# Combining pass of a sandwich layer: six buffers for the sums, loads two tiles ahead, and the inverse deviation taken as a ScalarE root and a VectorE reciprocal in place of GpSimd's power

## What is computed

```python
x = x + layernorm(mixer(layernorm(x)))            # first pass, gives x1
# experts: 8, two of them for each token, and a shared one
y = einsum('etd,te->td', experts(layernorm(x)), gate_dense) + shared(layernorm(x))
x = x + layernorm(y)                              # the second part is the combining pass
# layernorm: (x - mean) / sqrt(var + 1e-5), over the 256 channels
```

## Time and profile before

| what | us |
|---|---|
| median of three runs | 1092.72 |
| lowest and highest of the three | 1087.05, 1095.67 |
| the profiled execution's own time | 1095.33 |
| its span (first to last instruction) | 1093.5 |
| combining pass within the span | 1018.3 to 1093.5 |

### The profile page before, as it was taken

The page is one execution under the profiler, slowest core; times in us unless marked ns, Lnnn a source line. Parts: engine busy times, 40 slices in busy tenths (PEclk is TensorE's granted clock), DMA queues, the critical chain, the costliest instruction groups (busy, mean ns, idle before and its releaser), DMA issues. The chain is left out here.

```text
span 1093.5 us, 23369 instructions
## 1 busy us (share of the span) xinstructions
PE 978.0 (89%) x6344; PEld 874.3 (80%) x6344; DVE 863.2 (79%) x2223; ACT 574.5 (53%) x1045; POOL 763.3 (70%) x763
## 2 busy tenths in 40 slices
PE   4577999999999999999998979999999999997552
PEld 3466888888888888888887869899999999997331
DVE  5779999989989999899878657667777676666686
ACT  5335667556755765576555524344444443443465
POOL 3665787787778777877786634577776676667488
PEclk9879999999999999999999999999999999999555
DMA  6150453345334533443441476987787878986797
GB/s 218 40 161 31 141 165 106 124 142 163 90 132 149 158 94 133 149 143 100 143 131 54 141 258 134 257 181 117 116 171 156 213 120 211 224 200 85 254 395 287
DMA packets 107894, 171.93 MB, mean 157 GB/s; under 512 B 13870, under 2 KB 75977, under 8 KB 107593
## 3 DMA queue, kind: packets, MB, share of 16 engines
q1 hardware_dynamic: 76120, 119.68, 34.4%
q0 software_dynamic: 26976, 35.93, 18.8%
q10 hardware_dynamic: 4752, 15.80, 3.7%
HBM read 173.53 MB, written 76.08 MB: 228 GB/s over the span
## 5 line engine op out<-in xcount | busy, mean ns | idle before, releaser
L2063 POOL DMA_INDIRECT sum_y<-e_y,e_row_at x142 | 223.8, 1576 | 43.3 <-issue 39.8
L1897 PE MATMUL e_h_ps<-e_z_hi,w_room 128*128 128x256 f32 x1136 | 217.2, 284 | 11.6 <-DMA w_room<-w_split 9.4
L1897 PEld LDWEIGHTS e_h_ps<-e_z_hi,w_room 128*128 128x128 f32 x1136 | 181.8, 191 | 15.1 <-issue 13.4
L1941 ACT ACTIVATE e_act_h<-e_h_ps,w_room 128x256 f32<-128x256 f32 x142 | 67.4, 474 | 192.8 <-PE e_h_ps L1897 154.2
L1897 PE MATMUL e_h_ps<-e_z_lo,w_room 128*128 128x256 f32 x568 | 160.0, 282 | 0.0
L1647 POOL DMA_INDIRECT slots_x<-f_xf,f_at x120 | 127.6, 1063 | 29.0 <-issue 29.0
L1913 PE MATMUL e_y_ps<-w_room,e_h_hi 128*128 128x256 f32 x568 | 117.9, 291 | 1.8 <-DVE e_h_lo L1987 1.1
L1980 DVE SCALAR_TENSOR_TENSOR e_h<-e_h_ps,w_room,e_act_h 128x256 f32<-128x256 f32 x142 | 68.1, 482 | 61.8 <-ACT e_act_h L1941 48.6
L1172 DVE RECIPROCAL f_den<-f_den 128x256 f32<-128x256 f32 (+1 forms) x49 | 109.2, 2234 | 0.6
L1897 PEld LDWEIGHTS e_h_ps<-e_z_lo,w_room 128*128 128x128 f32 x568 | 108.5, 191 | 0.0
L651 PE MATMUL f_h_ps<-f_f_hi,f_w_hi 128*128 128x512 f32 x224 | 91.8, 410 | 6.0 <-DVE f_h_room L1208 3.2
(11 more groups left out here) (301 smaller groups left out, 2964.6 us busy)
## 6 DMA issues: line engine op xcount, KB each, us to landing
w_room<-w_split SPq DMA_DIRECT2D x73, 512.0 KB
w_room<-w_split SPq DMA_DIRECT2D x71, 514.0 KB
w_room<-w_split ACTq DMA_DIRECT2D x69, 512.0 KB
rows_room<-slots_x SPq DMA_DIRECT2D x71, 260.0 KB
f_x_in<-x SPq DMA_DIRECT2D x16, 512.0 KB, 5.2
f_x_res<-x SPq DMA_DIRECT2D x16, 512.0 KB, 4.6
x_dram<-f_x_room SPq DMA_DIRECT2D x16, 512.0 KB, 2.9
c_acc<-sum_y SPq DMA_DIRECT2D x16, 512.0 KB, 7.6
```

The source lines that it names most:

```text
L1897: last = pe.matmul(h_ps[q][:, which, :], w13(p, q, part)[:, which, c, :], z[p % 2][:, c, :], start=(n == 0), stop=(n == 5))
L1941: act.activation(act_h[q][:, :], h_ps[q][:, 0, :], ACT.Silu, bias=bias(p, 0, q)).then_inc(silu_ready, 1)
L2063: pool.indirect_dma_start(out=dst[:, :], out_offset=bass.IndirectOffsetOnAxis(ap=row_at[p][:, j:j + 1], axis=0), in_=y[p][:, j, :], in_off ...
```

## The change

All of it lies in `combine`, but for one tile and the names of semaphores in what comes before.

- `acc` has six buffers (`DEPTH`), `x1` and `res` have four (`X_DEPTH`). SyncE's queue first fetches `acc` of tiles 0 and 1, then in turn i `acc` of tile i+2 and `x1` of tile i. The load of `acc[s]` waits until tile s-6 is normalised.
- ScalarE takes `std = Sqrt(var + eps)` in a new `deviation`, which stands in turn i for tile i+1, between `gates_turned(i + 2)` and `normalise(i)`.
- VectorE takes the reciprocal and the offset in a new `scales`. Its turn i is `add(i)`, `scales(i - 1)`, `measure(i)`. Minus the mean and the variance plus epsilon as instructions of their own are gone.
- GpSimd keeps `add_x1` alone.
- `eps`, a 128 x 1 tile, is set by VectorE at the start of the expert stage; two semaphores there (`own_ready`, `gates_split`) become one (`prepared`).

```diff
-    DEPTH = 4
+    DEPTH, X_DEPTH = 6, 4
...
-            for i in range(tiles):
+            def load_acc(i):
+                if not inside(i, tiles):
+                    return
                 wait(sp, normed, i - DEPTH + 1)
                 sp.dma_start(acc[i % DEPTH][:, :, :], rows(acc_dram, i)).then_inc(acc_loaded[i % DEPTH], 16)
-                wait(sp, res_ready, i - DEPTH + 1)
-                sp.dma_start(x1[i % DEPTH][:, :, :], rows(x1_dram, i)).then_inc(x1_loaded[i % DEPTH], 16)
+            def load_x1(i):
+                wait(sp, res_ready, i - X_DEPTH + 1)
+                sp.dma_start(x1[i % X_DEPTH][:, :, :], rows(x1_dram, i)).then_inc(x1_loaded[i % X_DEPTH], 16)
+            for i in range(DEPTH - X_DEPTH):
+                load_acc(i)
+            for i in range(tiles):
+                load_acc(i + DEPTH - X_DEPTH)
+                load_x1(i)
...
+            def deviation(s):
+                if not inside(s, tiles):
+                    return
+                act.wait_ge(moments_ready, s + 1)
+                wait(act, rstd_ready, s - 1)
+                act.activation(std[s % 2][:, :], moments[s % 2][:, :, 1], ACT.Sqrt, bias=eps[:, :]).then_inc(std_ready, 1)
             for i in range(-2, tiles + 2):
                 gates_turned(i + 2)
+                deviation(i + 1)
                 normalise(i)
                 store(i - 1)
...
-                dve.wait_ge(moments_ready, s + 1)
-                wait(dve, offset_ready, s - 1)
-                dve.tensor_scalar(minus_mean[s % 2][:, :], moments[s % 2][:, :, 0], -1.0, None, ALU.mult)
-                dve.tensor_scalar(var[s % 2][:, :], moments[s % 2][:, :, 1], EPS, None, ALU.add)\
-                    .then_inc(var_ready, 1)
-            for i in range(tiles):
-                add(i)
+            def scales(s):
+                if not inside(s, tiles):
+                    return
+                dve.wait_ge(std_ready, s + 1)
+                wait(dve, normed, s - 1)
+                dve.reciprocal(rstd[s % 2][:, :], std[s % 2][:, :]).then_inc(rstd_ready, 1)
+                dve.wait_ge(rstd_ready, s + 1)
+                dve.scalar_tensor_tensor(out=offset[s % 2][:, :], in0=moments[s % 2][:, :, 0], scalar=-1.0,
+                                         in1=rstd[s % 2][:, :], op0=ALU.mult, op1=ALU.mult).then_inc(offset_ready, 1)
+            for i in range(tiles + 1):
+                if i < tiles:
+                    add(i)
+                scales(i - 1)
+                if i < tiles:
+                    measure(i)
...
-                pool.tensor_tensor(rstd[s % 2][:, :], var[s % 2][:, :], minus_half[:, :], ALU.pow)\
-                    .then_inc(rstd_ready, 1)
-                pool.wait_ge(rstd_ready, s + 1)
-                pool.tensor_tensor(offset[s % 2][:, :], minus_mean[s % 2][:, :], rstd[s % 2][:, :], ALU.mult)\
-                    .then_inc(offset_ready, 1)
...
-            for i in range(tiles + 1):
-                inverse_std(i)
-                add_x1(i - 1)
+            for i in range(tiles):
+                add_x1(i)
```

More of the change, by code:

```diff
@@ L1961, in _ @@
         def _(dve):
+            dve.memset(ahead["eps"][:, :], EPS)
             dve.tensor_tensor(own[:, :, :], tile_of["start"][:, :, None].to_broadcast([P, tiles, SUBS]),
-                              own_s[:, None, :].to_broadcast([P, tiles, SUBS]), ALU.add).then_inc(own_ready, 1)
+                              own_s[:, None, :].to_broadcast([P, tiles, SUBS]), ALU.add).then_inc(prepared, 1)
             for p in range(2):
                 dve.tensor_scalar(spare_row[p][:, :], own_s[:, :], float(TOKENS + p * T), None, ALU.add)\
-                    .then_inc(own_ready, 1)
-            dve.wait_ge(own_ready, 3)
+                    .then_inc(prepared, 1)
+            dve.wait_ge(prepared, 3)
             def low(s, p):
@@ L2095, in combine @@
         eye, b_out, b_ready = (ahead[n] for n in ("eye", "b_out", "b_ready"))
-        minus_half = sb("minus_half", [P, SUBS])
+        eps = ahead["eps"]
         gt = [sb(f"gt{p}", [G, T], F32R) for p in range(2)]
         acc = [sb(f"acc{p}", [P, SUBS, C]) for p in range(DEPTH)]
-        x1 = [sb(f"x1{p}", [P, SUBS, C]) for p in range(DEPTH)]
+        x1 = [sb(f"x1{p}", [P, SUBS, C]) for p in range(X_DEPTH)]
         normal = [sb(f"normal{p}", [P, SUBS, C]) for p in range(2)]
-        res = [sb(f"res{p}", [P, SUBS, C]) for p in range(DEPTH)]
+        res = [sb(f"res{p}", [P, SUBS, C]) for p in range(X_DEPTH)]
         stats = [sb(f"stats{p}", [P, SUBS, 6]) for p in range(2)]
         moments = [sb(f"moments{p}", [P, SUBS, 2]) for p in range(2)]
-        var = [sb(f"var{p}", [P, SUBS]) for p in range(2)]
-        minus_mean = [sb(f"minus_mean{p}", [P, SUBS]) for p in range(2)]
+        std = [sb(f"std{p}", [P, SUBS]) for p in range(2)]
         rstd = [sb(f"rstd{p}", [P, SUBS]) for p in range(2)]
@@ L2109, in combine @@
         b_ps = [ctx.enter_context(nc.psum_tensor(f"c_b_ps{p}", [P, SUBS, C], F32)) for p in range(2)]
-        x1_loaded = [sem(f"x1_loaded{p}") for p in range(DEPTH)]
-        half_ready = sem("half_ready")
+        x1_loaded = [sem(f"x1_loaded{p}") for p in range(X_DEPTH)]
         acc_loaded = [sem(f"acc_loaded{p}") for p in range(DEPTH)]
@@ L2124, in combine @@
         res_ready = sem("res_ready")
-        stored = [sem(f"stored{p}") for p in range(DEPTH)]
+        stored = [sem(f"stored{p}") for p in range(X_DEPTH)]
         block = ctx.enter_context(nc.Block())
@@ L2132, in _ @@
         def _(sp):
-            for i in range(tiles):
+            def load_acc(i):
+                if not inside(i, tiles):
+                    return
                 wait(sp, normed, i - DEPTH + 1)
                 sp.dma_start(acc[i % DEPTH][:, :, :], rows(acc_dram, i)).then_inc(acc_loaded[i % DEPTH], 16)
-                wait(sp, res_ready, i - DEPTH + 1)
-                sp.dma_start(x1[i % DEPTH][:, :, :], rows(x1_dram, i)).then_inc(x1_loaded[i % DEPTH], 16)
-            for p in range(DEPTH):
-                sp.wait_ge(stored[p], 16 * (tiles // DEPTH))
+            def load_x1(i):
[6 more added lines that the diff above has]
+                load_x1(i)
+            for p in range(X_DEPTH):
+                sp.wait_ge(stored[p], 16 * (tiles // X_DEPTH))
         @block.tensor
@@ L2189, in store @@
                 act.wait_ge(res_ready, s + 1)
-                act.dma_start(rows(out, s), res[s % DEPTH][:, :, :]).then_inc(stored[s % DEPTH], 16)
+                act.dma_start(rows(out, s), res[s % X_DEPTH][:, :, :]).then_inc(stored[s % X_DEPTH], 16)
+            def deviation(s):
[4 more added lines that the diff above has]
+                act.activation(std[s % 2][:, :], moments[s % 2][:, :, 1], ACT.Sqrt, bias=eps[:, :]).then_inc(std_ready, 1)
             for i in range(-2, tiles + 2):
                 gates_turned(i + 2)
+                deviation(i + 1)
                 normalise(i)
@@ L2203, in add, with measure @@
                 dve.tensor_tensor(here[:, :, :], b_ps[s % 2][:, :, :], here[:, :, :], ALU.add).then_inc(summed, 1)
+            def measure(s):
                 dve.wait_ge(summed, s + 1)
+                here = acc[s % DEPTH]
                 for j in range(SUBS):
```

27 lines of the change are left out of this document (10 added, 17 removed).

## The result

The changed kernel takes 1105.59 us (median; 1103.91 to 1106.56), the kernel before 1090.65 us in the same series. The ratio is 1.0146, with a 95% interval of 1.0112 to 1.018: slower, 15 us, where I had forecast 3 us less. Two of the kernels further down had one single run of over 2000 us (5325.84 and 2444.83 us), and their medians leave it out. The profiled execution has a span of 1104.5 us; its combining pass runs from the first load of the sums at 1017.08 us to the end, 87.4 us, where the pass before took 75.2 us (1018.26 to 1093.5).

A forecast was written before the change was run, and what follows sets the result against it. GpSimd and DMA were taken to bound the combining pass at 3.78 to 3.79 us a tile. After the head, six rings of 7.45 us gave a span 3.1 us shorter: 1089.6 against 1092.72 us, range 1083.5 to 1096.5.

The forecast's parts named there:

- the paragraph on VectorE: VectorE in the combining pass: addition to moments takes 3.27 us, with reciprocal and offset at 0.17 us each in between.
- The upper value that I gave for VectorE: VectorE's addition to moments with no overlap between instructions: 3.43 us instead of 3.27 us.
- GpSimd and the transfers as the old limits: Combining pass before the change: GpSimd and the DMA engines have the same pace, 3.78 to 3.79 us a tile.
- the late starts: GpSimd's power started 1.80 and 0.59 us late through waits for loads of sums; earlier loads were to remove this.
- The ring: Loop of waits over two tiles, moments i to moments i+2, through ScalarE, TensorE and VectorE: 7.45 us.
- The break-even: At 7.86 us for two tiles the ring equals GpSimd's old time; beyond that the change loses.
- The head and the table: First normalisation waits for moments 1, 1.6 us later; one table load for the root costs 0, at most 0.6 us.
- Rival 1: The ring has its upper values, 8.31 us for two tiles; span 3.0 us longer, 1095.7 us; chance 0.18.
- Rival 2: The ring does not bind, VectorE paces the start with 3.27 us; span 8 us shorter, 1084.5 us; chance 0.15.
- Rival 3: The root brings two table loads into each tile, 10.01 us for two tiles; 1107 us; chance 0.04.
- The range: Total time from 1083.5 to 1096.5 us, reaching from rival 2 to rival 1, widened by the spread of runs.
- the edits outside of the pass: In the expert stage, a memset and two semaphores made one: cost nothing, under cover of other work.

The follow-up runs named there:

- the buffers alone: Kernel before with six buffers for the sums, the new load order and the edits outside the combining pass: 1095.7 us, ratio 1.0016.
- The run with the longer ring: Changed kernel with moments in PSUM and a second, unread ScalarE copy of each tile of gates: 1096.86 us, ratio 1.0036.
- the runs with an opened ring and no hold: Changed kernel, moments in PSUM, with root after normalisation (1088.53 us, 0.995) or copies of gates one tile further ahead (1090.24 us, 0.9979).
- the last two runs: Kernel before with only the edits outside the combining pass (1092.05 us, ratio 1.0028), and kernel before unchanged (1091.42 us, ratio 1.0013).
- the run with the root behind: Changed kernel, moments in SBUF, with the root of tile i+1 after the normalisation of tile i: 1101.0 us, ratio 1.01.

## Why the prediction was wrong

**The step that failed** is in the paragraph on VectorE: "the offset I price like the small instruction on the same tile, 0.17 us". Seven of sixteen took 2.35 us. What the runs showed in place of that price is a wait for another engine: an offset that starts beside GpSimd's addition ends with it, and with one operand in PSUM it takes 0.16 us in the same place. I priced the instruction by its size, from a row in which GpSimd was idle: the small instruction of the earlier trace rows at 1028.33 ran before GpSimd's first addition, at 1029.88. In nine of the sixteen tiles that same line took 0.45 to 0.70 us. The upper value that I gave for VectorE, 3.43 us, was one without overlap, and did not cover this case; with it the bound would have been 3.27 + 2.35 - 0.16 = 5.46 us.

**GpSimd and the transfers as the old limits** fit the runs. With the buffers alone the late starts of the earlier trace rows are gone, and GpSimd kept 3.78 us a tile to the end.

**The ring** was right in kind and size: 7.45 us forecast, 7.36 measured with the hold gone, and 7.40 in the changed kernel less one hold. Term by term, from the rows of the run with the moments in PSUM: addition to moments 3.24 us (1042.17 to 1045.41) where I took 3.27; to the root 0.03 (0.05); root 0.16 (0.11); normalisations and store 1.97 (2.03); copy of gates with its handover 0.62 (0.64); product with its handover 1.34 (1.35). In the changed kernel the root has a pitch of 0.20 us (1058.87 to 1059.07). The store's issue ran inside the normalisations (1060.47 to 1060.83, inside ACTIVATEs from 1059.07 to 1061.14), as the reading of the earlier trace rows had it. The break-even that I gave, 7.86 us for two tiles, is a little low by my own terms: 7.45 + 3.1 / 6 is 7.97. The run with the longer ring, 7.85 us for two tiles, has a pass of 74.9 us, close to the 75.2 of before, and decides nothing between the two. What I did not see is that the ring also sets the place of the offset against GpSimd's addition. In every second tile VectorE waits 1.05 us for the product, and its offset then starts 0.02 us behind GpSimd.

**The head and the table** were forecast rightly. The rows of the changed kernel:

```profile
1019.64 1.28 ACT L2205 ACT_TABLE_LOAD   x1
...
1020.72 1.23 DVE L2219 TENSOR_TENSOR c_acc<-c_b_ps,c_acc 128x1024 f32<-128x1024 f32 x1 [13.57 <-DMA c_acc<-sum_y]
...
1023.83 0.30 ACT L2205 ACTIVATE c_std<-c_moments,c_eps 128x4 f32<-128x4 f32 x1 [2.90 <-DVE c_moments L2229]
...
1027.16 2.06 ACT L2190 ACTIVATE c_normal<-c_acc,c_offset,c_rstd 128x256 f32<-128x256 f32 x4
```

One table load, at 1019.64, in idle time. The first normalisation comes 6.44 us behind the first addition of VectorE; forecast 6.43, before 4.86.

**Rivals.** Rival 1 did not happen: the ring is not 8.31 us. Rival 2 did not either, as the ring binds; but its price, a span 8 us shorter, is near what the runs with an opened ring and no hold have, passes of 67.7 and 68.3 us against 75.2. Rival 3 gave 1107, near the measured 1105.6, by luck: its reason is not there, as there is one table load and not 32. The slower side had a mechanism that I had not listed, and a chance of 0.04 for it was too low.

**The range** ended at 1096.5 us. It was made of the bounds of terms I knew; the hold of one instruction by another engine was in none.

**The sum without the hold** fits the pass, within what single profiles can tell: 3.1 us less was forecast, and with the moments in PSUM it is 75.2 - 71.9 = 3.3 us against the first profile of the kernel before, 2.3 and 1.7 us against the other two of its pass. In the total no gain shows: 1.0007, and the interval (0.9983 to 1.0031) reaches only 1.9 us below no change. I had put the edits outside of the pass at nothing; whether they took back what the pass gained is what the last two runs leave open.

## What to carry to other kernels

When work moves from one engine to another, price it in rows where its new neighbours run, and look at the longest of a line as well as its mean: a small instruction that now and then ends with another engine's is held by it. A hold is cheap or dear by where it falls, and a loop of waits can put it on the same place in each turn; here one operand in PSUM removed it, and 0.3 us of added work on GpSimd removed nearly all of it. Read the length of the stage that was changed next to the total where the stages ahead vary by more than the gain.

## What was not expected of the hardware

- VectorE's SCALAR_TENSOR_TENSOR with both operands in SBUF, 128 x 4, takes 0.16 us alone and up to 2.37 us beside GpSimd's TENSOR_TENSOR of 2.35 us; with one operand in PSUM 0.16 us. It is held until 0.01 to 0.03 us after GpSimd's end.
- RECIPROCAL (0.17 us, at 1048.46 in the run with the root behind), aggregation (0.38 us) and an addition of PSUM and SBUF (1.22 us) kept their times beside the same GpSimd instruction. A TENSOR_SCALAR with one SBUF operand did not: 0.70 instead of 0.17 us in the kernel before. Why that one is held was not tried.
- ScalarE's root, 128 x 4 with a bias from a tile, takes 0.30 us, with 0.20 us to the next start; with its input in PSUM 0.26 us, with 0.16. The issue of a DMA (0.36 us) costs that queue nothing behind four ACTIVATEs: from their start to the next ACTIVATE it was 1.97 us with the issue (1059.07 to 1061.04) and 1.98 us without (1026.82 to 1028.80).
